# A four-layer GraphSAGE stack on one core: rests of a layer's first two chunks moved into the third place, PSUM banks that alternate by layer, and a layer's first loads ahead of the last stores

## Chip, core and metric

The kernel runs on one core of a Trainium2 chip. The metric is the device time of one execution in microseconds (us); lower is better. Engines are called by the names of the profile: PE (TensorE), PEld (its weight loads), DVE (VectorE), ACT (ScalarE), POOL (GpSimd) and SP (the engine whose queue issues almost all DMAs here).

## Reference

Input: node features x (3125 x 256, float32), 50000 edges (src, dst) and the weights of four layers. What is computed, cut to what matters:

```
def sage_conv(x, src, dst, Wl, Wr, b):
    agg = segment_sum(x[src], dst)          # sum over incoming edges
    deg = segment_sum(1, dst)
    return (agg / max(deg, 1)) @ Wl + x @ Wr + b

h = relu(layernorm(x))
h = relu(sage_conv(h, Wl1, Wr1, b1))        # 256 -> 256
h = relu(sage_conv(h, Wl2, Wr2, b2))        # 256 -> 128
h = relu(sage_conv(h, Wl3, Wr3, b3))        # 128 -> 256
return x + sage_conv(h, Wl4, Wr4, b4)       # 256 -> 256
```

## The kernel before

**Data.** The edges are first turned into a dense matrix of counts (source node by destination node, float16, resident in SBUF as `counts`). This is spread over the first half of the execution and runs into layer 1. From then on a layer's aggregation is a matrix product: `H` (features of all 25 tiles of 128 source nodes, in float16, a high and a low part) against `counts`. Layer 2 aggregates after its left map was already applied ("narrow"), so it has 128 features there.

**Chunks and places.** The destination nodes are cut into seven chunks: six of 512 nodes and a last one of 53. They are worked through in `ORDER` = 5, 6, 4, 3, 2, 1, 0; the position in that order is called place q (0 to 6). So place 0 is a full chunk, place 1 is the short chunk of 53 nodes, and places 2 to 6 are full chunks. For one place PE issues 25 tiles of sums (`add_sources`, L1720): two matmuls a tile (high and low part) in layers 2 and 3, four in layer 4, each with 512 columns, or 53 in place 1. They accumulate in one of two PSUM banks, `agg_ps` (bank 0) or `window_ps` (bank 1). Before the change, places 0, 2, 4, 6 use bank 0 and places 1, 3, 5 use bank 1, in each of layers 2 to 4; layer 1 uses bank 0 throughout.

**The rest of a place.** What follows a place's sums is called its rest:

- DVE multiplies the sums by 1/degree into `aggT` (`scale_agg`, L1200). It needs the tile `rdeg`, loaded from DRAM for each place, and `aggT` free, that is the map of the place before done.
- PE applies the layer's map (`lin`: L1682 in layers 2 and 3, L1665 in layer 4) to `aggT` and to `selfT`, the chunk's own features, loaded from DRAM (`load_self`, L642).
- In layer 2, DVE adds the sums to the map (L1301). ACT applies bias and relu into `newT` (L1412); SP stores `newT` to DRAM (`store_new`, L663).
- In layers 2 and 3 ACT makes the float16 high part (L1425), DVE the low part (L1207), PE transposes both (`turn`, L1707; once in layer 2, twice in layer 3), DVE copies the result to `newH` (`copy_turned`, L1219), and SP stores it (`store_H`, L670) for the next layer's `H`.
- In layer 4, DVE adds x (L1289) and SP stores the output.

PE has one in-order stream, written out by hand: the map and turn of place q-1 stand among the sums of place q, after fixed tiles. `rest(l, q)` lists them: map after tile 6, turn after tile 18 in layer 2; map after 6, turns after 16 and 22 in layer 3; map after tile 4 in layer 4. With this rule the rest of place 0 stands among the 53-column sums of place 1, and the rest of place 1 among those of place 2.

**Change of layer.** Place 0 of a layer consumes the `H` that the layer before has made. Its 25 tiles are taken in `ORDER`, and the rest of the last place of the old layer stands among them (`REST_AT`, the map before tile 0). SP issues, in this order: reload of `H` for all chunks but the last one (after all sums of the old layer, L745); `store_new` and `store_H` of place 6; the reload of the last chunk of `H` (L750), once its store has landed; then, once every `hT_stored` of the old layer is there, `load_self(0)` (L642), `load_rdeg(0)` (L648), and in layer 2 six late weight loads (`Wr2`, `Wl3`, `Wr3`, `b4`, `Wl4`, `Wr4`: L719 to L725), which all count on one semaphore, `late_loaded`. The map of place 0 in layer 2 waits for all six.

After that, `after(q)` on SP waits for the map of place q, then issues `load_self(q+1)`, `load_rdeg(q+1)` (once `agg_scaled` allows), `store_new(q)` and `store_H(q)`.

Of the kernel before, what the change touches and what calls it, by code (L numbers as in the profile page):

```python
# [26 lines left out]
def sage_stack_kernel(nc, x, src, dst, Wl1, Wr1, b1, Wl2, Wr2, b2, Wl3, Wr3, b3, Wl4, Wr4, b4, out):  # L27
# [13 lines left out]
    P = 128  # L41
# [3 lines left out]
    NT = -(-N // P)  # L45
# [4 lines left out]
    NCH = NFULL + 1  # L50
# [106 lines left out]
    for at_, (w, i) in enumerate(STEP):  # L157
        if i:
            continue
        k = STEPS[w]  # L160
# [62 lines left out]
    with ctx:  # L223
# [6 lines left out]
        def sem(name):  # L230
            return ctx.enter_context(nc.semaphore(name))
# [221 lines left out]
        degree_done = sem("degree_done")  # L453
        degree_inverted = sem("degree_inverted")
        degree_turned = sem("degree_turned")
        late_loaded = sem("late_loaded")
        rdeg_made = sem("rdeg_made")
        rdeg_stored = sem("rdeg_stored")
# [35 lines left out]
        CONSTS = CONSTS_TURN + 9  # L494
        LATE_KEYS = sum(r[4] > 1 for r in RUNS)
        LATE_CONSTS = len(FOURS) + 1
        LATE = 16 * 6
        x4 = newH[:, :, :, :].rearrange("p t h f -> p (t h f)").bitcast(f32).rearrange("p (t f) -> p t f", t=TPC)
        FULL = (CH, TPC)
        LAST = (TAIL, 1)  # L500
# [15 lines left out]

            return full * q - (full - last if not isinstance(q, int) or q > 1 else 0)

        def over_places(eng, do):

            do(1, 1)
            do(2, 0)
            with eng.Fori(1, NCH // 2) as i:
                do(2 * i + 1, 1)
                do(2 * i + 2, 0)

        def chunk_cols(c, n):
            return bass.ds(c * CH, n)
# [56 lines left out]
        def _(sp):  # L585
# [45 lines left out]
                store_h0T(j)  # L631

            for l in (1, 2, 3, 4):
                if l > 1:
                    sp.wait_ge(hT_stored[l - 1], 16 * NCH)

                def load_self(q):
                    c = chunk_at(q)
                    n, t = size_of(c)
                    if l == 1 and isinstance(q, int) and q <= 2:  # L640
                        wait_h0T(sp, *((q,) if q < 2 else ()))
                    sp.dma_start(selfT[:, 0:SELF[l], 0:n], hT_d[l - 1][:, 0:SELF[l], chunk_cols(c, n)]  # L642
                                 ).then_inc(self_loaded[l], 16)

                def load_rdeg(q):
                    c = chunk_at(q)
                    n, t = size_of(c)
                    sp.dma_start(rdeg[:, 0:n], rdeg_d[0:1, chunk_cols(c, n)].broadcast_to([P, n])  # L648
                                 ).then_inc(rdeg_loaded[l], 16)
# [34 lines left out]
                def load_x4(q):  # L684
# [4 lines left out]
                    else:  # L689
                        sp.dma_start(x4[0:n, 0, :], x[c * CH:N, :]).then_inc(x4_loaded, 16)  # L690

                def after(q, last=False):

                    sp.wait_ge(lin_done[l], both(q + 1, LIN[l], 1 if l == 4 else LIN[l]))
                    if not last:
                        load_self(q + 1)
                        if l > 1:
                            sp.wait_ge(agg_scaled[l], AGG[l] * (q + 1))
                            load_rdeg(q + 1)
                    if l == 1 and isinstance(q, int) and q == 0:  # L700
                        for j in range(3, NCH):
                            store_h0T(j)
                    if l < 4:
                        store_new(q)
                        store_H(q)
                    else:
                        store_out(q)
                        if not last:
                            load_x4(q + 1)

                load_self(0)
                if l > 1:
                    if l == 2:
                        sp.wait_ge(rdeg_stored, 16 * NCH)
                    load_rdeg(0)
                if l == 2:


                    sp.dma_start(Wr2_sb, Wr2.rearrange("(k p) n -> p k n", p=P)).then_inc(late_loaded, 16)  # L719
                    for i, w in enumerate((Wl3, Wr3)):  # L720
                        sp.dma_start(W3[:, i, :], w).then_inc(late_loaded, 16)
                    sp.dma_start(b4rows, b4.rearrange("(o n) -> o n", o=1).broadcast_to([P, D])
                                 ).then_inc(late_loaded, 16)
                    for i, w in enumerate((Wl4, Wr4)):
                        sp.dma_start(W14[:, i, :, :], w.rearrange("(k p) n -> p k n", p=P)  # L725
                                     ).then_inc(late_loaded, 16)
# [142 lines left out]
        def _(dve):  # L869
# [423 lines left out]
            for l in (2, 3, 4):  # L1293
                def place(q, bank):
                    n, t = size_of(chunk_at(q))
                    scale_agg(l, q, bank)
                    if l == 2:
                        dve.wait_ge(lin_done[2], q + 1)
                        if not isinstance(q, int) or q > 0:
                            dve.wait_ge(hT_stored[2], 16 * q)  # L1300
                        v.tensor_tensor(newT[:, 1, 0:n], lin_ps[:, 0, 0:n], aggT[:, 0, 0:n], ALU.add  # L1301
                                        ).then_inc(summed, 1)
                    for h in range(TURNS[l]):
                        low_part(l, q, h)
                        copy_turned(l, q, h)
                    if l == 4:
                        add_out(q)

                place(0, 0)
                over_places(dve, place)  # L1310


        @block.scalar
        def _(act):
# [193 lines left out]
            for l in (2, 3):  # L1508
                def place(q, bank):
                    relu(l, q)  # L1510
                    for h in range(TURNS[l]):
                        high_part(l, q, h)

                place(0, 0)
                over_places(act, place)


        @block.tensor
        def _(pe):
# [128 lines left out]
            def lin(l, q):  # L1648
# [2 lines left out]
                pe.wait_ge(agg_scaled[l], AGG[l] * (q + 1))  # L1651
                pe.wait_ge(self_loaded[l], 16 * (q + 1))
                if l == 2 and isinstance(q, int) and q == 0:
                    pe.wait_ge(late_loaded, LATE)
                if l == 4:
                    if not isinstance(q, int) or q > 0:
# [163 lines left out]
            def rest(l, q):  # L1820
# [3 lines left out]
                        3: {6: [lambda: lin(3, q)], 16: [lambda: turn(3, q, 0)], 22: [lambda: turn(3, q, 1)]},  # L1824
                        4: {4: [lambda: lin(4, q)]}}[l]


            for l in (2, 3, 4):
                def place(q, bank):
                    between = rest(l, q - 1)  # L1830

                    if not isinstance(q, int) or q > 1:
                        pe.wait_ge(agg_scaled[l], AGG[l] * (q - 1))
                    for k in range(NT):
                        add_sources(l, q, bank, k, k == 0, k == NT - 1)
                        for do in between.get(k, []):
                            do()

                pe.wait_ge(agg_scaled[l - 1], AGG[l - 1] * NCH)
                tiles = [(c, k) for c in ORDER for k in range(c * TPC, min((c + 1) * TPC, NT))]
                left = [do for _, dos in sorted(rest(l - 1, NCH - 1).items()) for do in dos]
                for i, (c, k) in enumerate(tiles):
                    if i in REST_AT[l - 1]:
                        left.pop(0)()
                    pe.wait_ge(H_loaded[c], 16 * (l - 1))
                    add_sources(l, 0, 0, k, i == 0, i == NT - 1)
                over_places(pe, place)
            lin(4, NCH - 1)  # L1850


# [21 lines left out]
```

## Time and profile before

| what | value |
|---|---|
| median of 3 runs | 731.82 us (731.35 to 734.61) |
| the profiled execution's own time | 732.57 us |
| its span in the profile | 730.5 us |
| mean granted PE clock | 0.975 |
| PE busy | 671.8 us, 92% of the span |
| DVE, ACT, POOL busy | 292.2, 172.4, 31.1 us |
| layers 2, 3 and 4, start of place 1 to start of place 3 | 363.84 to 390.86, 457.27 to 480.69, 570.10 to 603.97 us |

How to read it: the profiled execution is a single one, with a span 2.07 us shorter than its own time and a time 0.75 us above the median. "Busy" for PE counts matmuls whose ends are modelled, so the distance from one start to the next is the better measure of what a matmul costs. Positions are in us from the start of the span. A granted clock of 1.00 is 2.4 GHz and 0.50 is 1.2 GHz. Layer 2's place 0 starts near 350 us, and layers 2 to 4 take the rest of the span.

### The profile page before, as it was taken

Reading aid. Unit: us, or ns where it says so; the run is one execution under the profiler, and the core shown is the slowest. Engines: PE = TensorE matmul, PEld = TensorE weight load, DVE = VectorE, ACT = ScalarE, POOL = GpSimd, SP = SyncE. Lnnn points to the kernel's source line nnn. Section 1 sums busy time; section 2 is a strip of 40 time slices with the busy share of each in tenths; the row PEclk is TensorE's granted clock in tenths of the full one; section 3 lists DMA queues with packets and bytes.
Section 4 is the critical chain, followed back from the end, with each engine's and each line's share of the span. In section 5 each row is a group of like instructions: output and inputs, shape, how many; then the busy total and the mean of one; then the engine's idle time right before and its main releaser. Section 6 shows DMA issues by size and latency. Waiting matters only on the chain.

```text
span 730.5 us, 11548 instructions
## 1 busy us (share of the span) xinstructions
PE 671.8 (92%) x4545; PEld 366.5 (50%) x4546; DVE 292.2 (40%) x826; ACT 172.4 (24%) x339; POOL 31.1 (4%) x80
## 2 busy tenths in 40 slices
PE   5578898999999999999959999899989999999997
PEld 4234555655554555644434444444434646556464
DVE  6898866686767757601011221212221101001001
ACT  4844753363624503210101010111120000000000
POOL 7000000000000000000000000000000110110110
PEclk9999999899999999999979999999999999999999
DMA  8000012300101001064423235222346222130230
GB/s 260 18 2 1 30 61 89 108 1 6 58 17 56 13 8 58 17 14 112 132 83 106 87 106 185 81 78 87 115 138 212 81 78 63 39 102 20 80 100 29
DMA packets 39425, 53.50 MB, mean 73 GB/s; under 512 B 8558, under 2 KB 21519, under 8 KB 39377
## 3 DMA queue, kind: packets, MB, share of 16 engines
q1 hardware_dynamic: 39260, 52.59, 23.5%
q8 instruction: 33, 0.54, 0.3%
q10 hardware_dynamic: 116, 0.24, 0.1%
q14 instruction: 16, 0.12, 0.1%
HBM read 31.86 MB, written 20.97 MB: 72 GB/s over the span
## 4 chain that ended last, share of the span: by engine, by line
PE 84%; DVE 7%; ACT 3%; DMA 3%; issue 2%; POOL 1%; SPq 1%; DVEq 0%; POOLq 0%; ACTq 0%
PE agg_ps L1720 39%; PE window_ps L1720 12%; PE lin_ps L1643 6%; PE window_ps L1599 6%; PE lin_ps L1665 6%; PE lin_ps L1682 4%; PE lin_ps L1739 2%; DVE early L1146 2%; PE turn_ps L1707 2%; PE lin_ps L1690 2%; ACT counts L1373 1%; DMA H_d<-newH 1%; DMA W<-in_L_gnn_Wr_dram 1%; DMA H<-H_d 1%; PE degree_ps L1751 1%
## 5 line engine op out<-in xcount | busy, mean ns | idle before, releaser
L1720 PE MATMUL agg_ps<-counts,H 128*128 128x512 f16 (+2 forms) x1500 | 355.0, 374 | 2.1 <-DMA H<-H_d 2.1
L1720 PEld LDWEIGHTS agg_ps<-counts,H 128*128 128x128 f16 x1500 | 130.0, 99 | 119.1 <-issue 12.9
L1146 DVE TENSOR_TENSOR early<-early 128x512 f16<-128x512 bf16 (+2 forms) x466 | 153.6, 390 | 38.6 <-PE window_ps L1599 37.2
L1373 ACT ACTIVATE counts<-window_ps 128x400 f16<-128x400 f32 x196 | 96.3, 505 | 133.5 <-PE window_ps L1599 129.6
L1599 PEld LDWEIGHTS window_ps<-early 128*128 128x128 f16 x892 | 70.0, 100 | 112.7 <-issue 30.7
L1599 PE MATMUL window_ps<-early 128*128 128x100 f16 (+1 forms) x892 | 100.3, 223 | 24.4 <-DVE early L1146 14.3
L1720 PE MATMUL window_ps<-counts,H 128*128 (+1 forms) x600 | 96.2, 316 | 0.0
L1720 PEld LDWEIGHTS window_ps<-counts,H 128*128 128x128 f16 x600 | 45.6, 98 | 49.6 <-issue 4.1
L1200 DVE SCALAR_TENSOR_TENSOR aggT<-agg_ps,columns,rdeg 128x512 f32<-128x512 f32 (+1 forms) x30 | 20.5, 715 | 101.1 <-PE agg_ps L1720 89.8
L835 POOL TENSOR_TENSOR newH<-newH,early 128x256 f32<-128x256 f32 (+1 forms) x25 | 17.4, 725 | 680.9 <-DMA newH<-in_x_dram 680.9
L1219 DVE COPY newH<-turn_ps 128x1024 f16<-128x1024 f16 (+1 forms) x28 | 17.7, 632 | 58.6 <-PE turn_ps L1707 58.6
L1412 ACT ACTIVATE newT<-lin_ps,columns 128x512 f32<-128x512 f32 (+1 forms) x28 | 17.3, 633 | 96.9 <-PE lin_ps L1682 62.8
L1207 DVE SCALAR_TENSOR_TENSOR partsT<-newT,columns,partsT 128x512 f16<-128x512 f32 (+1 forms) x21 | 14.4, 684 | 53.6 <-ACT partsT L1425 53.0
L1682 PE MATMUL lin_ps<-selfT,early 128*128 128x512 f32 (+1 forms) x56 | 26.8, 583 | 6.8 <-DMA W<-in_L_gnn_Wr_dram 5.8
L1289 DVE TENSOR_TENSOR newT<-lin_ps,newH 128x512 f32<-128x512 f32 (+1 forms) x13 | 8.7, 671 | 56.4 <-PE lin_ps L1665 51.3
L1665 PE MATMUL lin_ps<-W,aggT 128*128 128x256 f32 (+1 forms) x100 | 25.9, 382 | 1.7 <-DVE aggT L1200 1.7
L1643 PE MATMUL lin_ps<-aggT,W 128*128 128x512 f32 (+1 forms) x56 | 25.8, 565 | 1.4 <-DVE aggT L1200 1.4
L1665 PE MATMUL lin_ps<-W,selfT 128*128 128x256 f32 (+1 forms) x100 | 25.7, 379 | 0.0
L1643 PE MATMUL lin_ps<-selfT,W 128*128 128x512 f32 (+1 forms) x56 | 25.5, 561 | 0.0
L1412 ACT ACTIVATE newT<-newT,columns 128x512 f32<-128x512 f32 (+1 forms) x7 | 4.7, 667 | 83.8 <-DVE newT L1301 83.8
L1200 DVE SCALAR_TENSOR_TENSOR aggT<-window_ps,columns,rdeg 128x512 f32<-128x512 f32 (+1 forms) x12 | 6.8, 589 | 39.9 <-PE window_ps L1720 36.7
L1707 PE MATMUL turn_ps<-ident,partsT 128*128 128x128 f16 (+1 forms) x200 | 16.5, 225 | 6.6 <-DVE partsT L1207 6.6
(159 smaller groups left out, 381.2 us busy)
## 6 DMA issues: line engine op xcount, KB each, us to landing
selfT<-hT_d SPq DMA_DIRECT2D x18, 512.0 KB, 4.3
hT_d<-newT SPq DMA_DIRECT2D x12, 512.0 KB, 4.2
rdeg<-rdeg_d SPq DMA_DIRECT2D x18, 256.0 KB, 4.2
counts<-in_x_dram SPq DMA_DIRECT2D x6, 512.0 KB, 8.3
hT_d<-counts SPq DMA_DIRECT2D x6, 512.0 KB, 3.2
H_d<-newH SPq DMA_DIRECT2D x12, 256.0 KB, 2.0
H<-H_d SPq DMA_DIRECT2D x12, 256.0 KB, 4.2
H_d<-newH SPq DMA_DIRECT2D x6, 512.0 KB, 2.6
```

The costliest lines, as they stand in the source:

```text
L835: nc.gpsimd.tensor_tensor(x4[0:q, i, :], x4[0:q, i, :], b4rows[0:q, :], ALU.add).then_inc(x4_biased, 1)
L1146: last = v.tensor_tensor(hot[:, group % GROUPS, 0:n * size].rearrange("p (r n d) -> p r n d", r=n, d=2), numbers_to[:, 0:size].rearrange(" ...
L1200: v.scalar_tensor_tensor(out=aggT[:, h, 0:n], in0=(agg_ps, window_ps)[bank][:, h, 0:n], scalar=unscale[:, l - 1:l], in1=rdeg[:, 0:n], op0= ...
L1219: v.tensor_copy(to, turn_ps[0:rows_, 0:2 * t, :].rearrange("p (t a) f -> p t a f", a=2)).then_inc(turn_copied[l], 1)
L1373: a.activation(counts[:, :, 2 * w * WIN:2 * (w + 1) * WIN].rearrange("p t (a w) -> p a t w", a=2), window_ps[:, FILL_AT[w] % 2, 0:2 * KEYS ...
L1412: a.activation(newT[:, h, 0:n], source, ACT.Relu, bias=bT[:, bias + h:bias + h + 1]).then_inc(relu_done[l], 1)
L1599: m(window_ps[:, at % 2, key0:key0 + keys], hot_src[:, group % GROUPS, r * P:(r + 1) * P], hot_key[:, group % GROUPS, r * keys:(r + 1) * k ...
L1643: last = m(lin_ps[:, h, 0:n], W14[:, i // 2, i % 2, h * P:(h + 1) * P], (aggT, selfT)[i // 2][:, i % 2, 0:n], start=(i == 0), stop=(i == 3))
L1665: last = m(lin_ps[0:rows_, g, i * D:(i + 1) * D], h, w, start=(j == 0), stop=(j == len(ops) - 1))
L1682: last = m(lin_ps[:, h, 0:n], w, r, start=(i == 0), stop=(i == len(ops) - 1))
L1707: last = nc.tensor.transpose(turn_ps[0:rows_, 2 * i + part, :], partsT[:, part, i * P:i * P + rows_], ident16[:, :])
L1720: last = m((agg_ps, window_ps)[bank][:, h, 0:n], H_of[:, k, part, h * P:(h + 1) * P], counts[:, k, chunk_cols(c, n)], start=first and part ...
```

## The change

What it does:

- **Rests of places 0 and 1.** In layers 2 to 4, place 1 has only its sums. The rest of place 0 and that of place 1 both stand among the sums of place 2, after the tiles that the new `first_rests` lists. From place 3 on nothing changes.
- **Banks.** `FIRST_BANK` gives the bank of places 0, 2, 4, 6 for each layer: 1 in layer 2, 0 in layer 3, 1 in layer 4. So the first place of a layer does not use the bank of the last place of the layer before. The wait ahead of place 0 asks for all scaled places of the old layer but the last; the wait for the last stands ahead of place 1. `REST_AT` is as before: the old layer's last map stands before tile 0 and waits for the last scaled place itself.
- **First loads.** `load_self(0)` and `load_rdeg(0)` of the next layer are issued in `first_loads`, after the last map of the old layer and ahead of `store_new(6)` and `store_H(6)`. For layer 2 the load of `Wr2` goes with them and has its own semaphore, `wr2_loaded`; the map of place 0 in layer 2 waits for that alone, and the five other late loads are waited for by the first map of layer 3.

The diff, cut where only a parameter is passed on:

```
+        wr2_loaded = sem("wr2_loaded")
...
-        LATE = 16 * 6
+        LATE = 16 * 5
...
-        def over_places(eng, do):
-
-            do(1, 1)
-            do(2, 0)
+        FIRST_BANK = [0, 0, 1, 0, 1]
+
+        def over_places(eng, do, first):
+
+            do(1, 1 - first)
+            do(2, first)
             with eng.Fori(1, NCH // 2) as i:
-                do(2 * i + 1, 1)
-                do(2 * i + 2, 0)
+                do(2 * i + 1, 1 - first)
+                do(2 * i + 2, first)
...
             for l in (1, 2, 3, 4):
-                if l > 1:
-                    sp.wait_ge(hT_stored[l - 1], 16 * NCH)
...
+                def first_loads(l):
+
+                    sp.wait_ge(hT_stored[l - 1], 16 * (NCH - 1))
+                    load_self(0, l)
+                    if l == 2:
+                        sp.wait_ge(rdeg_stored, 16 * NCH)
+                        sp.dma_start(Wr2_sb, Wr2.rearrange("(k p) n -> p k n", p=P)).then_inc(wr2_loaded, 16)
+                    sp.wait_ge(agg_scaled[l - 1], AGG[l - 1] * NCH)
+                    load_rdeg(0, l)
+
                 def after(q, last=False):
 
                     sp.wait_ge(lin_done[l], both(q + 1, LIN[l], 1 if l == 4 else LIN[l]))
+                    if last and l < 4:
+                        first_loads(l + 1)
                     if not last:
...
-                load_self(0)
-                if l > 1:
-                    if l == 2:
-                        sp.wait_ge(rdeg_stored, 16 * NCH)
-                    load_rdeg(0)
+                if l == 1:
+                    load_self(0)
+                else:
+                    sp.wait_ge(hT_stored[l - 1], 16 * NCH)
                 if l == 2:
 
 
-                    sp.dma_start(Wr2_sb, Wr2.rearrange("(k p) n -> p k n", p=P)).then_inc(late_loaded, 16)
...
                 pe.wait_ge(self_loaded[l], 16 * (q + 1))
                 if l == 2 and isinstance(q, int) and q == 0:
+                    pe.wait_ge(wr2_loaded, 16)
+                if l == 3 and isinstance(q, int) and q == 0:
                     pe.wait_ge(late_loaded, LATE)
...
+            def first_rests(l):
+
+                return {2: {2: [lambda: lin(2, 0)], 8: [lambda: turn(2, 0, 0)],
+                            13: [lambda: lin(2, 1)], 19: [lambda: turn(2, 1, 0)]},
+                        3: {2: [lambda: lin(3, 0)], 8: [lambda: turn(3, 0, 0)], 12: [lambda: turn(3, 0, 1)],
+                            15: [lambda: lin(3, 1)], 19: [lambda: turn(3, 1, 0)], 22: [lambda: turn(3, 1, 1)]},
+                        4: {2: [lambda: lin(4, 0)], 10: [lambda: lin(4, 1)]}}[l]
 
             for l in (2, 3, 4):
                 def place(q, bank):
                     between = rest(l, q - 1)
+                    if isinstance(q, int):
+                        between = first_rests(l) if q == 2 else {}
 
                     if not isinstance(q, int) or q > 1:
                         pe.wait_ge(agg_scaled[l], AGG[l] * (q - 1))
+                    else:
+                        pe.wait_ge(agg_scaled[l - 1], AGG[l - 1] * NCH)
                     for k in range(NT):
                         add_sources(l, q, bank, k, k == 0, k == NT - 1)
                         for do in between.get(k, []):
...
-                pe.wait_ge(agg_scaled[l - 1], AGG[l - 1] * NCH)
+                pe.wait_ge(agg_scaled[l - 1], AGG[l - 1] * (NCH - 1))
...
-                    add_sources(l, 0, 0, k, i == 0, i == NT - 1)
-                over_places(pe, place)
+                    add_sources(l, 0, FIRST_BANK[l], k, i == 0, i == NT - 1)
+                over_places(pe, place, FIRST_BANK[l])
```

## Rows read from the trace of the kernel before

**Rows 1.** The page's first part: busy time, share of the span, instructions.

```profile
PE 671.8 (92%) x4545; PEld 366.5 (50%) x4546; DVE 292.2 (40%) x826; ACT 172.4 (24%) x339; POOL 31.1 (4%) x80
```

**Rows 2.** Who waited for whom: us in total, times, longest.

```profile
PE lin_ps L1682 <- DMA W<-in_L_gnn_Wr_dram: 5.8, 1, 5.8
PE turn_ps L1707 <- DVE partsT L1207: 6.6, 4, 2.5
```

**Rows 3.** Timeline of PE, layer 2: start, us, instruction, [idle before].

```profile
363.84 0.51 PE L1720 MATMUL window_ps<-counts,H 128*128 128x53 f16 x14
370.12 3.75 PE L1682 MATMUL lin_ps<-selfT,early 128*128 128x512 f32 x4 [5.77 <-DMA W<-in_L_gnn_Wr_dram]
...
376.95 0.88 PE L1707 MATMUL turn_ps<-ident,partsT 128*128 128x128 f16 x8 [2.48 <-DVE partsT L1207]
...
390.86 3.19 PE L1720 MATMUL window_ps<-counts,H 128*128 x14
...
403.81 3.19 PE L1720 MATMUL agg_ps<-counts,H 128*128 x14
```

**Rows 4.** Chain that ended last, layer 2: start, us, what.

```profile
373.90 0.70 DVE newT L1301
...
382.54 0.38 PE lin_ps L1682 x4
...
388.10 0.23 PE turn_ps L1707 x2
...
395.76 5.18 PE window_ps L1720 x24
```

**Rows 5.** Timeline of PE, layer 3.

```profile
457.27 0.52 PE L1720 MATMUL window_ps<-counts,H 128*128 128x53 f16 x14
...
464.23 0.62 PE L1707 MATMUL turn_ps<-ident,partsT 128*128 128x128 f16 x8 [1.67 <-DVE partsT L1207]
...
466.51 1.03 PE L1707 MATMUL turn_ps<-ident,partsT 128*128 128x128 f16 x8 [1.36 <-DVE partsT L1207]
...
480.69 3.18 PE L1720 MATMUL window_ps<-counts,H 128*128 x14
...
495.81 3.19 PE L1720 MATMUL agg_ps<-counts,H 128*128 x14
```

**Rows 6.** Chain that ended last, layers 3 and 4.

```profile
457.54 0.76 DVE aggT L1200
...
471.59 0.83 PE lin_ps L1682 x8
...
578.57 2.01 PE window_ps L1720 x80
...
584.90 1.86 PE lin_ps L1665 x8
```

**Rows 7.** Timeline of PE, layer 4.

```profile
570.10 0.67 PE L1720 MATMUL window_ps<-counts,H 128*128 128x53 f16 x20
...
603.97 4.48 PE L1720 MATMUL window_ps<-counts,H 128*128 x20
...
632.46 4.48 PE L1720 MATMUL agg_ps<-counts,H 128*128 x20
```

**Rows 8.** Windows: length, busy of each engine, PEclk, DMA share, GB/s.

```profile
367.00:369.00 2.00, 0.00 (x0) 0.00 (x0) 0.00 (x0) 0.00 (x0) 0.00 (x0) 0.50 0.58 201
...
444.00:450.00 6.00, 5.94 (x30) 2.63 (x30) 1.49 (x3) 1.44 (x2) 0.00 (x0) 1.00 0.87 268
```

**Rows 9.** Timeline at the change from layer 2 to 3.

```profile
450.67 0.34 SPq L670 DMA_DIRECT2D H_d<-newH  x1
...
455.53 1.41 PEld L1720 LDWEIGHTS agg_ps<-counts,H 128*128 128x128 f16 x8 [0.50 <-DMA H<-H_d]
```

**Rows 10.** The page's DMA issues: count, KB each, us to landing.

```profile
hT_d<-newT SPq DMA_DIRECT2D x6, 256.0 KB, 4.0
rdeg<-rdeg_d SPq DMA_DIRECT2D x3, 26.5 KB, 3.1
```

More of the change, by code:

```diff
@@ L633, in _, with load_self @@
             for l in (1, 2, 3, 4):
-                if l > 1:
-                    sp.wait_ge(hT_stored[l - 1], 16 * NCH)
-                def load_self(q):
+                def load_self(q, l=l):
                     c = chunk_at(q)
@@ L643, in load_self, with load_rdeg @@
                                  ).then_inc(self_loaded[l], 16)
-                def load_rdeg(q):
+                def load_rdeg(q, l=l):
                     c = chunk_at(q)
@@ L1307, in place @@
                         add_out(q)
-                place(0, 0)
-                over_places(dve, place)
+                place(0, FIRST_BANK[l])
+                over_places(dve, place, FIRST_BANK[l])
         @block.scalar
@@ L1512, in place @@
                         high_part(l, q, h)
-                place(0, 0)
-                over_places(act, place)
+                place(0, FIRST_BANK[l])
+                over_places(act, place, FIRST_BANK[l])
         @block.tensor
```

## The prediction, made before the changed kernel ran

> **What bounds the kernel now.** I read the page's busy shares first: PE works 92% of the span, the next engine 40% [rows 1]. So the end comes earlier only where PE waits or runs slowly, or if it gets less to do. The change gives PE the same matmuls in another order, so the gain can only come from waits and from the clock. The list of waits then says which waits: PE stood 5.8 us once before a map of L1682, until a weight load had landed, and 6.6 us in four places before turns, until DVE had made the low part [rows 2]. The timeline says where. The 5.77 us lie 14 matmuls into place 1 of layer 2, and a wait of 2.48 us before the turn follows in the same place [rows 3]. Two more waits before turns, 1.67 and 1.36 us, lie in place 1 of layer 3 [rows 5]. All this is in place 1, whose sums have 53 columns: in layer 4, 80 of them take 2.01 us [rows 6], 25.1 ns each, against 5.18 us for 24 sums of 512 columns, 0.216 us each [rows 4]. So the 50 sums of place 1 in layer 2 or 3 last 1.26 us, and a map's rest of over 3 us cannot hide in them. In place 2, a tile of two sums lasts 0.43 us and 25 tiles 10.8 us. The reader is to see that a wait's cover is the length of the sums behind which it stands.
>
> **Layer 2.** From the start of place 1 to that of place 3 the kernel takes 390.86 - 363.84 = 27.02 us [rows 3]. What has to be done there: the 50 short sums, 1.26 us; a full place with one full map and turn, for which the distance between the next two places stands, 403.81 - 390.86 = 12.95 us [rows 3]; the short map, 0.38 us, and the short turn, 0.23 us [rows 4]. Together 14.82 us. The excess is 12.2 us: 5.77 + 2.48 of it PE stood idle, and the other 3.95 us are work that took longer than elsewhere. The clock says why: 0.50 of full, that is 1.2 GHz, inside the idle stretch [rows 8], and not back to 2.4 GHz at once. I expect both idle and slow parts to go.
>
> What takes their place: the map of place 0 now stands after tile 2 of place 2, the turn after tile 8. From the map's end (DVE's add starts 0.02 us behind it, at 373.90) to the turn at 376.95, the chain add, relu, high part, low part needed 3.05 us [rows 3, 4]. Six tiles cover 2.59 us. So a stall of 0.46 us stays. After: 14.82 + 0.46 = 15.28 us, a gain of 11.7 us.
>
> This holds only if the loads come in time. `Wr2`, `selfT` and `rdeg` of place 0 are now issued about 10 us earlier, behind the old layer's last map, and I count no wait for them. The map of place 1 stands after tile 13, 0.46 us stall, a turn and 11 tiles (4.7 us) behind the first map, over 5.5 us. Its `rdeg` needs two issues on SP's queue and 3.1 us to land [rows 10]; it fits with about 1 us to spare. DVE's add for place 1 must also wait until `newT` of place 0 is stored: relu ends about 1.5 us behind the map, the store lands 4.0 us later [rows 10], 5.5 us, against a short map that ends near 6.1 us. It fits, by 0.6 us. `rdeg` and `selfT` of place 2 are asked for only after tile 13, about 5 us ahead of the place's end; should they be late by a microsecond, the next map stands six tiles further on (3 us), so it costs nothing; without that cover it would cost its full lateness.
>
> **Layer 3.** Before: 480.69 - 457.27 = 23.42 us. After: 1.26 + 15.12 (480.69 to 495.81) [rows 5] + 0.83 for the short map [rows 6] + two short turns at 0.23 [rows 4] = 17.67 us. The first turn stands six tiles behind the map and needs less than in layer 2, as no add is in the chain. The two full turns stood 466.51 - 464.23 = 2.28 us apart when PE only waited [rows 5]; now four tiles (1.73 us) and the turn itself lie between. The stall is between 0 and 0.55 us; the turn fills most of it, and I take 0.1. A gain of 5.65 us.
>
> **Layer 4.** Before: 603.97 - 570.10 = 33.87 us; after: 2.51 for 100 short sums + 28.49 (603.97 to 632.46) [rows 7] + 1.86 for the short map [rows 6] = 32.86 us, a gain of 1.0 us. A tile here has four sums (0.86 us), so eight tiles between the maps cover the output's add.
>
> **Does place 2 start at once?** It waits for the scaled sums of place 0. In layer 3 DVE was done with them 457.54 + 0.76 - 457.27 = 1.03 us after place 1 had begun [rows 5, 6], and place 1 now lasts 1.26 us. No stall, by 0.2 us; in layer 4 there are two such operations and 2.5 us.
>
> **Banks.** Nothing. The old layer's last map still stands ahead of tile 0 and waits for the last scaled place itself, so PE stands there as before. The bound is zero from both sides: the matmuls are the same, and `window_ps` is free by then.
>
> **First loads on SP's queue and in the DMA engines.** Each change of layer now has `selfT` and `rdeg` (and `Wr2`) ahead of `store_new(6)` and `store_H(6)`, 0.77 MB. SP's own issue time is no matter: `store_H(6)` waits longer for its turn. But the bytes lie ahead of it. At the change from 2 to 3, the six windowed microseconds from 444 moved 1.61 MB at 268 GB/s and kept the DMA engines 0.87 busy [rows 8]; with 0.77 MB more they would be done at 444 + 2.38 / 0.268 = 452.9 us, behind the issue of `store_H(6)` at 450.67 [rows 9]. The last chunk's reload follows only on that store, and PE already stood 0.5 us in its weight loads for it [rows 9], so lateness is paid in full. Below: 0 us (the queue is drained as fast as it fills; then these 0.5 us might even go). Above: all of 0.77 MB at 268 GB/s, 2.9 us. I take 1.2 us, since 2.2 us of the backlog lie behind the issue of the store, and about one of these would have passed before its own bytes start. At the other two changes the store is issued longer after the reloads, and I take nothing there, with the same 2.9 us as upper bound.
>
> The Trainium skill, DMA: Bandwidth & Descriptors, section Queues, rings and completion order, says that an engine takes the descriptors of one ring in order and lands a semaphore's increment only after all its earlier writes. That speaks against putting the loads first: by it the store could not be reported ahead of them, and the 1.2 us would not be 0. No row here shows the two transfers in that order.
>
> **Sum.** 11.7 + 5.65 + 1.0 - 1.2 = 17.2 us. The profiled execution took 732.57 us, so 715.4; the median of the runs is 731.82, which gives 714.6. I say 715.0.
>
> **Rivals.**
> - *Late reload at each change of layer.* 2.9 us three times, in place of 1.2: 17.2 - 7.5 = 9.7 us gained, 722 us; partly, 717 to 722. For it: the 0.5 us that PE already stood; against: the first and third change leave room. 12%.
> - *The chains still stall in place 2.* Place 2 has two rests in one place and DVE takes both in order; the margins above are 0.6 and 1 us. If layer 2 keeps its 2.48 us instead of 0.46 and layer 3 its 3.03 instead of 0.1: 4.9 us less, 720; partly, 717 to 720. 10%.
> - *The clock falls at each place 1 for a short time*, since PE now has a run of short matmuls there and a place begins without a map. Layer 2's excess of slow work, 3.95 us, in all three layers: 727. Against: short sums ran at 25.1 ns in layer 4 and the next place at full speed. 4%.
> - *Nothing to be measured.* Both of the first two at their upper ends and some clock: 17.2 - 7.5 - 4.9 - 4 = 1, 731 to 732. 3%.
> - *Slower.* One mechanism: the clock stays at 1.2 GHz through place 2. Work that lasts 12.95 and 15.12 us in layers 2 and 3 would last twice that: 28 us more, 743. It decides once more than 17.2 us of full-speed work runs at half. For it: after the long idle it was at 0.50 [rows 8]. Against: that idle is what goes, and the page shows none as long elsewhere in these layers. 5%.
>
> The Trainium skill, TensorE: Matmul & The Clock Gate, Part 1, says the slow clock is the default and activity releases it. It is the rule behind the last rival; the trace agrees in so far as the idle stretch ends at 0.50.
>
> **How the numbers follow.** My forecast, 712 to 718, has 66%. The range 712 to 720 takes in the bounds of the stalls, the second rival and a third of the first: 66 + 10 + 4 = 80%. About 0.5% is what a measurement of this kernel can tell from no change, so under 728.2 is faster: 66 + 12 + 10 + 4 = 92%; same 3%; slower 5%.
>
> **What the profile after would show.** Layer 2, place 1 to 3: about 15.3 us and no wait for a weight load; layer 3: 17.8; layer 4: 32.9; 50 short sums in about 1.3 us; a stall near 0.5 us before the first turn of layer 2's place 2; granted clock 1.00 at both places; PE waiting for `H<-H_d` some 1.2 us longer near the end of layer 3's place 0. I would be wrong if the clock fell all the same, if PE waited before tile 0 of place 2, or if the reload were late everywhere.

## The result and the profile after

The changed kernel took 716.24 us (median of 4 runs, 714.76 to 716.84), the kernel before, on the same chip, 733.11 us (median of 4, 731.35 to 734.61). The ratio is 0.9763, 95% interval 0.9731 to 0.9796: 2.4% faster, and 1.2 us above the 715.0 that were forecast. The profiled execution has a span of 713.8 us against 730.5, 16.7 us less; the prediction's sum was 17.2.

The busy shares on the page after, beside [rows 1]:

```profile
PE 664.6 (93%) x4545; PEld 363.3 (51%) x4546; DVE 292.6 (41%) x826; ACT 172.3 (24%) x339; POOL 30.8 (4%) x80
```

PE has the same 4545 matmuls, in 7.2 us less busy time. So only part of the 16.7 us is idle time; most of the rest is work that ran faster. (A small part is bookkeeping: the modelled end of the last matmul ahead of a wait lies about 0.16 us behind the point where the next one would have started, so each wait that goes takes that much "busy" time with it.)

PE's timeline in layer 2 after; it answers to [rows 3]:

```profile
363.85 1.42 PE L1732 MATMUL agg_ps<-counts,H 128*128 128x53 f16 x50
365.11 1.45 PE L1732 MATMUL window_ps<-counts,H 128*128 128x512 f16 x6
366.40 1.88 PE L1694 MATMUL lin_ps<-selfT,early 128*128 128x512 f32 x4
368.12 2.75 PE L1732 MATMUL window_ps<-counts,H 128*128 128x512 f16 x12
371.36 0.62 PE L1719 MATMUL turn_ps<-ident,partsT 128*128 128x128 f16 x8 [0.49 <-DVE partsT L1217]
...
379.44 3.19 PE L1732 MATMUL agg_ps<-counts,H 128*128 x14
```

Place 1 is one run of 50 short sums, 1.26 us from its start to that of place 2. The map starts without a wait, and the one wait left is 0.49 us before the turn. From place 1 to place 3: 379.44 - 363.85 = 15.59 us, where 27.02 us stood.

The granted clock in the windows of the same stretch (columns as in [rows 8]), where the kernel before had 0.50:

```profile
367.00:369.00 2.00, 2.00 (x8) 0.71 (x8) 0.68 (x1) 0.00 (x0) 0.00 (x0) 1.00 0.00 0
369.00:371.00 2.00, 1.87 (x9) 0.66 (x7) 0.46 (x2) 1.44 (x2) 0.00 (x0) 1.00 0.23 61
371.00:373.00 2.00, 1.64 (x14) 1.05 (x15) 1.21 (x3) 0.00 (x0) 0.00 (x0) 1.00 0.30 110
```

PE's timeline in layer 3 and 4 after, beside [rows 5, 7]:

```profile
432.41 1.95 PE L1694 MATMUL lin_ps<-selfT,early 128*128 128x512 f32 x4 [0.99 <-DVE aggT L1210]
...
445.23 1.90 PE L1732 MATMUL agg_ps<-counts,H 128*128 128x512 f16 x8 [1.23 <-DMA H<-H_d]
446.97 1.41 PE L1732 MATMUL window_ps<-counts,H 128*128 128x53 f16 x50
...
464.93 3.19 PE L1732 MATMUL window_ps<-counts,H 128*128 x14
...
554.34 2.68 PE L1732 MATMUL agg_ps<-counts,H 128*128 128x53 f16 x100
556.86 2.75 PE L1732 MATMUL window_ps<-counts,H 128*128 128x512 f16 x12
...
587.31 4.48 PE L1732 MATMUL agg_ps<-counts,H 128*128 x20
```

Layer 3, place 1 to 3: 464.93 - 446.97 = 17.96 us. Layer 4: 587.31 - 554.34 = 32.97 us. In layer 3, too, part of what went is slow work, which the prediction doesn't mention. In the trace of before, after the waits of 1.67 and 1.36 us, the clock was at 0.50, and 14 sums of place 2 took 471.43 - 467.54 = 3.89 us, where they take 3.02 at full speed:

```profile
467.54 4.04 PE L1720 MATMUL agg_ps<-counts,H 128*128 128x512 f16 x14
471.43 0.32 PE L1682 MATMUL lin_ps<-aggT,early 128*128 128x53 f32 x2
...
467.00:469.00 2.00, 2.00 (x14) 1.12 (x12) 0.87 (x2) 0.00 (x0) 0.00 (x0) 0.50 0.00 0
```

The line at 445.23 is the cost: eight sums on H's last chunk waited 1.23 us for its reload.

### The profile page after: what moved, and what is told of

Its sections match the earlier page's. It is cut to its first block, busy times and chain, and to the rows that moved or that the text cites. A ratio compares the mean times of both kernels' runs of the same rounds, so it can differ in the third digit from the quotient of the medians.

```text
span 713.8 us, 11549 instructions
## 1 busy us (share of the span) xinstructions
PE 664.6 (93%) x4545; PEld 363.3 (51%) x4546; DVE 292.6 (41%) x826; ACT 172.3 (24%) x339; POOL 30.8 (4%) x80
## 4 chain that ended last, share of the span: by engine, by line
PE 85%; DVE 7%; ACT 3%; DMA 3%; issue 2%; POOL 0%; DVEq 0%; SPq 0%; ACTq 0%; POOLq 0%
PE agg_ps L1732 32%; PE window_ps L1732 20%; PE lin_ps L1653 6%; PE window_ps L1609 6%; PE lin_ps L1677 6%; PE lin_ps L1694 4%; PE lin_ps L1751 2%; DVE early L1156 2%; PE turn_ps L1719 2%; PE lin_ps L1702 2%; ACT counts L1383 1%; DMA H<-H_d 1%; DMA H_d<-newH 1%; PE degree_ps L1763 1%; PE degree_ps L1533 1%
## 5 line engine op out<-in xcount | busy, mean ns | idle before, releaser
L1732 PE MATMUL agg_ps<-counts,H 128*128 128x512 f16 (+2 forms) x1350 | 290.3, 349 | 1.2 <-DMA H<-H_d 1.2
L1732 PE MATMUL window_ps<-counts,H 128*128 (+2 forms) x750 | 157.9, 366 | 1.9 <-DMA H<-H_d 1.9
L1732 PEld LDWEIGHTS agg_ps<-counts,H 128*128 128x128 f16 x1350 | 104.7, 99 | 81.5 <-issue 9.3
L1732 PEld LDWEIGHTS window_ps<-counts,H 128*128 128x128 f16 x750 | 68.9, 98 | 84.7 <-issue 4.4
L1210 DVE SCALAR_TENSOR_TENSOR aggT<-agg_ps,columns,rdeg 128x512 f32<-128x512 f32 (+1 forms) x27 | 17.0, 659 | 67.5 <-PE agg_ps L1732 61.9
L1229 DVE COPY newH<-turn_ps 128x1024 f16<-128x1024 f16 (+1 forms) x28 | 17.7, 633 | 51.6 <-PE turn_ps L1719 51.6
L1210 DVE SCALAR_TENSOR_TENSOR aggT<-window_ps,columns,rdeg 128x512 f32<-128x512 f32 (+1 forms) x15 | 10.4, 716 | 68.0 <-PE window_ps L1732 68.0
L1694 PE MATMUL lin_ps<-selfT,early 128*128 128x512 f32 (+1 forms) x56 | 24.9, 547 | 1.0 <-DVE aggT L1210 1.0
L1677 PEld LDWEIGHTS lin_ps<-W,aggT 128*128 128x128 f32 (+1 forms) x100 | 18.6, 187 | 5.1 <-DVE aggT L1210 1.6
```

What stands on the lines that cost most here:

```text
L1210: v.scalar_tensor_tensor(out=aggT[:, h, 0:n], in0=(agg_ps, window_ps)[bank][:, h, 0:n], scalar=unscale[:, l - 1:l], in1=rdeg[:, 0:n], op0= ...
L1229: v.tensor_copy(to, turn_ps[0:rows_, 0:2 * t, :].rearrange("p (t a) f -> p t a f", a=2)).then_inc(turn_copied[l], 1)
L1677: last = m(lin_ps[0:rows_, g, i * D:(i + 1) * D], h, w, start=(j == 0), stop=(j == len(ops) - 1))
L1694: last = m(lin_ps[:, h, 0:n], w, r, start=(i == 0), stop=(i == len(ops) - 1))
L1732: last = m((agg_ps, window_ps)[bank][:, h, 0:n], H_of[:, k, part, h * P:(h + 1) * P], counts[:, k, chunk_cols(c, n)], start=first and part ...
```

## Experiments

Of every run, the time from one stage to the next is compared, because the part ahead of the change moves from one execution to the next: layer 1's last map starts between 342.4 and 347.1 us in the traces of kernels that are the same up to there. Columns of this table: the distance from place 1 to place 3 in layers 2, 3 and 4; the last map of layer 2 to place 1 of layer 3 (place 0 of layer 3 with its waits); layer 1's last map to the end of the span; all in us. Then the median and its ratio to the kernel before, which ran beside each group of runs again (medians 732.43 to 733.25 us). In "last map later" the map itself moves, so the two columns that count from it are left open.

| run | L2 | L3 | L4 | place 0 of L3 | to the end | median | ratio (95%) |
|---|---|---|---|---|---|---|---|
| before | 27.02 | 23.42 | 33.87 | 13.44 | 387.2 | 733.11 | 1 |
| after | 15.59 | 17.96 | 32.97 | 14.56 | 370.3 | 716.24 | 0.9763 (0.9731 to 0.9796) |
| rests back | 20.09 | 23.51 | 33.88 | 13.83 | 380.7 | 726.78 | 0.9915 (0.9899 to 0.9932) |
| loads back | 19.29 | 17.97 | 32.97 | 13.59 | 373.4 | 717.42 | 0.9782 (0.9762 to 0.9801) |
| loads back, one semaphore | 18.45 | 17.97 | 32.98 | 13.40 | 372.1 | 720.47 | 0.9824 (0.9806 to 0.9842) |
| banks back | 15.58 | 17.97 | 32.98 | 14.33 | 370.2 | 718.33 | 0.9804 (0.9782 to 0.9827) |
| loads behind at 2 to 3 | 15.59 | 17.97 | 32.98 | 13.39 | 369.1 | 715.21 | 0.9768 (0.9743 to 0.9792) |
| and turn at 10 | 14.92 | 17.97 | 32.97 | 13.35 | 368.4 | 715.37 | 0.9769 (0.9749 to 0.979) |
| last map later | 15.58 | 17.98 | 32.97 | - | - | 726.97 | 0.9934 (0.991 to 0.9958) |
| more bytes ahead | 15.59 | 17.97 | 32.97 | 15.97 | 371.7 | 717.67 | 0.979 (0.9768 to 0.9812) |
| after, again | 15.59 | 17.96 | 32.97 | 13.69 | 369.5 | 715.95 | 0.977 (0.9743 to 0.9797) |
| behind, turn at 10, early reload | 15.08 | 17.97 | 32.97 | 13.14 | 368.0 | 713.21 | 0.9743 (0.9718 to 0.9769) |

### Rests back

```
-                    if isinstance(q, int):
-                        between = first_rests(l) if q == 2 else {}
```

> The changed kernel with the rests of places 0 and 1 back at their old tiles (place 0's among place 1's short sums); first loads and banks stay changed. Theory 'cover' (a rest costs what the sums behind which it stands do not hide): layer 2, place 1 to 3, about 17.9 us (14.8 of work, 0.7 for the scaled sums, 2.45 before the turn), up to 20 if the clock falls; layer 3 back at 23.4, layer 4 at 33.9. Together 8.6 us over the changed kernel: about 725 us, 1 to 1.5% faster than before. Rival 'the weight load was all': the moved rests carry nothing, 716 us as the changed kernel.

Measured: 726.78 us, 0.85% faster than the kernel before, less than the 1 to 1.5% expected. Layer 3 and 4 are back at 23.51 and 33.88 us, layer 2 at 20.09, the upper end of what was expected. PE's timeline of layer 2:

```profile
365.51 1.99 PE L1694 MATMUL lin_ps<-selfT,early 128*128 128x512 f32 x4 [0.56 <-DVE aggT L1210]
367.34 0.77 PE L1732 MATMUL agg_ps<-counts,H 128*128 128x53 f16 x24
370.58 0.62 PE L1719 MATMUL turn_ps<-ident,partsT 128*128 128x128 f16 x8 [2.48 <-DVE partsT L1217]
371.04 0.47 PE L1732 MATMUL agg_ps<-counts,H 128*128 128x53 f16 x12
371.34 4.87 PE L1732 MATMUL window_ps<-counts,H 128*128 128x512 f16 x14
```

And its windows:

```profile
371.00:373.00 2.00, 2.00 (x21) 0.91 (x19) 0.96 (x2) 0.00 (x0) 0.00 (x0) 0.60 0.28 104
373.00:375.00 2.00, 2.00 (x7) 0.78 (x6) 0.00 (x0) 0.00 (x0) 0.00 (x0) 0.55 0.24 93
```

The 2.48 us before the turn are back to the hundredth, though no load is waited for: this wait is the chain's length less the sums that stand in between. The clock fell after it, and the 14 sums that follow took from 371.34 to the next map at 376.05, 4.71 us, against 3.02 us at full speed [14 x 0.216, rows 4]. The rival "the weight load was all" falls. The early loads alone (with the new banks, which "banks back" shows to do nothing) save layer 2 6.9 us (27.02 to 20.09) and the others nothing.

### Loads back

```
                     sp.wait_ge(lin_done[l], both(q + 1, LIN[l], 1 if l == 4 else LIN[l]))
-                    if last and l < 4:
-                        first_loads(l + 1)
...
                     sp.wait_ge(hT_stored[l - 1], 16 * NCH)
+                    first_loads(l)
```

> The changed kernel with the first loads of a layer issued where they were, behind the last stores and the last reload of H; Wr2 keeps its own semaphore. Theory 'cover': rdeg of layer 2's place 0 lands near 366 us, so place 2 there starts about 1.7 us late; the reload wait at the change from 2 to 3 falls from 1.2 to about 0.4 us. Net +0.6 us: about 717 us. Rival 'the early loads carry the layer-2 gain': PE waits 5 us or more again in layer 2 and the clock falls, 722 us or more. Rival 'the reload wait has nothing to do with the loads ahead of it': it stays at 1.2 us.

Measured: 717.42 us. Layer 3's place 0 is 1.0 us shorter, with a wait for H of 0.19 us in place of 1.23, if the changed kernel's first trace is taken; its second trace has 13.69 us and 0.23, and against that nothing is gained. Layer 2 is 3.7 us longer than after, not 1.7. PE's timeline:

```profile
364.57 1.41 PE L1731 MATMUL agg_ps<-counts,H 128*128 128x53 f16 x50
367.83 2.55 PE L1731 MATMUL window_ps<-counts,H 128*128 128x512 f16 x6 [1.85 <-DVE aggT L1209]
370.17 2.53 PE L1693 MATMUL lin_ps<-selfT,early 128*128 128x512 f32 x4
```

and the window:

```profile
369.00:371.00 2.00, 2.00 (x5) 0.85 (x4) 0.00 (x0) 0.00 (x0) 0.00 (x0) 0.50 0.16 56
```

The late `rdeg` costs about the wait that was expected: 1.85 us, or 2.0 from start to start (3.26 us between the places where 1.26 are needed). The other 1.7 us are the clock at 0.50: six sums took 2.34 us from start to start in place of 1.29, the map 2.37 in place of 1.72. So the expected 717 us was met by luck: from layer 1's last map to the end the trace is 3.1 us longer than that of the changed kernel, where 0.6 was expected. The traced execution was also the slowest of the four (719.33 us; the others 715.25 to 717.94) and had the lowest mean clock (0.980; the others 0.985 to 0.988), so the clock need not have fallen like this in the others.

### Loads back, and all late loads on the wait

```
                     pe.wait_ge(wr2_loaded, 16)
+                    pe.wait_ge(late_loaded, LATE)
```

> As the run with the loads back, and layer 2's first map waits for all late weight loads again. So only the rests and banks are changed. Theory 'cover': the map waits until about 370 us in place of 368, 1.9 us more than with the loads back; layer 2, place 1 to 3, about 19.2 us, 719 us in all; if the clock falls as before the change, up to 4 us more, 723. Rival 'each byte of the 5.77 us wait comes back': 722.5 plus the clock's 4, 726 us.

Measured: 720.47 us in the timed runs; in its trace layer 2 took 18.45 us, less than the run above:

```profile
370.24 1.47 PE L1732 MATMUL window_ps<-counts,H 128*128 128x512 f16 x6 [1.30 <-DVE aggT L1209]
372.87 1.96 PE L1694 MATMUL lin_ps<-selfT,early 128*128 128x512 f32 x4 [1.16 <-DMA W<-in_L_gnn_Wr_dram]
```

The wait for the weights is 1.16 us, near a fifth of the 5.77 us [rows 3], on the same loads. Not all of the difference is cover. The loads landed 5.34 us after the start of place 1 (372.87 - 367.53), against 6.28 before; of these PE spent 1.26 us on the sums of place 1 and 1.29 on three tiles of place 2, and it stood 1.30 us for the scaled sums, which need the late `rdeg`. So PE stood 2.46 us in two waits where it stood 5.77 in one. The clock stayed at 1.00 in every window from 363 to 379. The rival "each byte of the wait comes back" falls. The medians (720.5 against 717.4 us) and the traces (372.1 against 373.4 us to the end) order these two runs differently; one trace of each can't tell how often the clock falls in either. The medians don't decide it: in this run's trace layer 1's last map starts at 347.10 us, in the run's above at 344.11, so 3.0 us lie ahead of everything that the two runs differ in. The 719 us expected were near the 720.47 for that reason; layer 2 itself was 0.75 us shorter than expected.

### Banks back

```
-        FIRST_BANK = [0, 0, 1, 0, 1]
+        FIRST_BANK = [0, 0, 0, 0, 0]
...
-                pe.wait_ge(agg_scaled[l - 1], AGG[l - 1] * (NCH - 1))
+                pe.wait_ge(agg_scaled[l - 1], AGG[l - 1] * NCH)
```

> The changed kernel with bank 0 for places 0, 2, 4, 6 in every layer and the old wait ahead of place 0. Theory: the banks do nothing, since the old layer's last map stands ahead of tile 0 and waits for the same scaled place: 716 us, the waits before the last maps stay at 1.37, 0.99 and 0.96 us. Rival: the banks save the wait for the last scaled place, about 1 us at each change of layer: 719 us.

Measured: 718.33 us, 2 us over the changed kernel, with intervals that overlap. The stages decide: 370.2 us to the end against 370.3. The waits ahead of the three last maps are 1.37, 0.99 and 0.96 us in both kernels; two of them:

```profile
434.59 1.96 PE L1694 MATMUL lin_ps<-selfT,early 128*128 128x512 f32 x4 [0.99 <-DVE aggT L1210]
...
528.49 1.10 PE L1694 MATMUL lin_ps<-aggT,early 128*128 128x512 f32 x2 [0.96 <-DVE aggT L1210]
```

The banks alone do nothing, as the map in front of tile 0 waits for the same scaled place.

### The last map later

So that the banks could pay, the old layer's last map and turns were put two tiles later.

```
-        REST_AT = {1: (0, 4, 9), 2: (0, 8), 3: (0, 7, 11)}
+        REST_AT = {1: (2, 6, 11), 2: (2, 10), 3: (2, 9, 13)}
```

> The changed kernel, but the old layer's last map and turns stand two tiles later in place 0 (map after 2 tiles, turns shifted as well), so that the alternated banks could hide the wait for the last scaled place. Theory 'H is the limit': PE can't begin tile 0 until H's first chunk is reloaded, 4 us after the sums end; the map no longer fills that time, and the last chunk's store and reload come later by two tiles' time. Layer 2's, 3's and 4's place 0 each 1 to 3 us longer: 719 to 723 us. Rival 'banks pay once the map is moved': 1 us less at each change of layer, 713 us.

Measured: 726.97 us, ratio 0.9934 (0.991 to 0.9958). PE's timeline at the three changes of layer:

```profile
344.70 1.02 PE L1732 MATMUL window_ps<-counts,H 128*128 128x512 f16 x4 [2.85 <-DMA H<-H_d]
...
436.57 1.02 PE L1732 MATMUL agg_ps<-counts,H 128*128 128x512 f16 x4 [3.05 <-DMA H<-H_d]
...
535.41 3.57 PE L1732 MATMUL window_ps<-counts,H 128*128 128x512 f16 x8 [6.39 <-DMA H<-H_d]
```

Nobody waits for the scaled sums any more, and all wait for H: 2.85, 3.05 and 6.39 us. At the first two changes of layer this costs 2.4 us and 1.3 to 2.2 us (against the changed kernel's two traces), as expected. At the third it costs 6.9 us: behind the longest wait the clock was at 0.50, eight sums took 3.36 us from start to start and the map 2.74, 2.7 us more than at full speed, and the other 4.2 us are longer waits, beyond the 1 to 3 us expected. Behind the waits of 2.85 and 3.05 us the four sums took 0.86 us from start to start, full speed. The map in front of tile 0 fills the reload's time, and this is why the banks can't pay here.

### Bytes ahead of the last store: none, as after, and double

Three kernels on one question: does PE's wait for H's last chunk in layer 3's place 0 come from the loads that the change put ahead of `store_H(6)`? In the first, they go behind the reload at this one change of layer:

```
-                    if last and l < 4:
+                    if last and l in (1, 3):
                         first_loads(l + 1)
...
+                if l == 3:
+                    first_loads(l)
```

> The changed kernel, but at the change from layer 2 to 3 selfT and rdeg are loaded behind the last reload of H, as before the change. Theory 'bytes ahead': the last chunk's store and reload no longer queue behind 0.52 MB, PE's wait for the reload falls from 1.23 to about 0.1 us; rdeg still lands before place 1 begins, since place 0 ends 4 us later. 1.1 us off: about 715 us. Rival 'rdeg is late': place 2 of layer 3 starts 1 us late and nothing is won. Rival 'the wait comes from elsewhere': 1.23 us stays.

In the second, two more loads of 256 KB into halves that layer 3 doesn't use stand ahead:

```
                     load_rdeg(0, l)
+                    if l == 3:
+                        sp.dma_start(selfT[:, 1:2, 0:CH], hT_d[2][:, 0:1, chunk_cols(ORDER[0], CH)]
+                                     ).then_inc(extra_loaded[0], 16)
+                        sp.dma_start(aggT[:, 1:2, 0:CH], hT_d[2][:, 0:1, chunk_cols(ORDER[0], CH)]
+                                     ).then_inc(extra_loaded[1], 16)
```

> The changed kernel with 0.52 MB more (two unused loads of 256 KB into free halves) ahead of the last stores at the change from layer 2 to 3; the loads are extra work that the reference doesn't need. Theory 'bytes ahead': PE's wait for the last chunk of H in layer 3's place 0 grows by 0.52 MB at about 270 GB/s, 1.9 us, from 1.23 to 3.1 us: about 718 us, and the clock may fall. Rival 'fixed cost': the wait stays near 1.2 us, however many bytes are ahead.

The third is the changed kernel once more:

> The changed kernel once more, unaltered, beside the next run on the same chip. Theory: 716 us, PE's wait for H's last chunk at the change from 2 to 3 between 0.4 and 1.3 us, as it lay in the runs with the same bytes ahead (1.23, 0.44, 0.90). If it is 0 here, the bytes ahead are not its cause.

SP's timeline shows it best: `store_H(6)` (L670 or L671) is issued, and the reload (L760 and its like) goes out once that store has landed. First the loads behind:

```profile
438.36 0.34 SPq L670 DMA_DIRECT2D H_d<-newH  x1
440.40 0.34 SPq L762 DMA_DIRECT2D H<-H_d  x1
```

The changed kernel, its first trace:

```profile
434.48 0.38 SPq L642 DMA_DIRECT2D selfT<-hT_d  x1
434.90 0.43 SPq L648 DMA_DIRECT2D rdeg<-rdeg_d  x1
435.88 0.34 SPq L663 DMA_DIRECT2D hT_d<-newT  x1
439.14 0.34 SPq L670 DMA_DIRECT2D H_d<-newH  x1
442.53 0.34 SPq L760 DMA_DIRECT2D H<-H_d  x1
```

Its second trace:

```profile
438.11 0.34 SPq L670 DMA_DIRECT2D H_d<-newH  x1
440.57 0.34 SPq L760 DMA_DIRECT2D H<-H_d  x1
```

Double the bytes:

```profile
439.80 0.34 SPq L671 DMA_DIRECT2D H_d<-newH  x1
444.48 0.34 SPq L769 DMA_DIRECT2D H<-H_d  x1
```

From the store's issue to the issue of the reload, which SP sends as soon as the store has landed: 2.04 us with nothing ahead, as before the change (452.71 - 450.67; its first number is in [rows 9]); 3.39 and 2.46 us with 0.52 MB; 4.68 us with 1.04 MB. PE's wait follows: none, 1.23, 0.23 and 2.56 us (3.1 were expected for the last). "Rests back" and "banks back", whose queue is the same here, lie in between: 2.57 us with a wait of 0.44, 3.06 with 0.90. So the bytes are the cause and the wait is not fixed; but the same 0.52 MB cost anything between 0.2 and 1.2 us, which the one forecast number didn't say. What counts is what is still under way when the store is issued: in the changed kernel's first trace `rdeg` landed at 441.2 us, 2.1 us after the store's issue, in the second at 439.2, 1.1 us after it. In "last map later" the same two loads are ahead of the store, but they were issued 5.6 us after the reload of `H` began in place of 2.8, and the store took 2.03 us, as with nothing ahead. Moving the loads behind costs layer 3 nothing, 17.97 us. "Loads behind" has the ratio 0.9768, where the changed kernel has 0.9763 and 0.977: timing can't tell them apart. The gain is read from the stage, place 0 of layer 3: 13.39 us against 14.56 and 13.69.

### The turn two tiles later, and an earlier reload

With the loads behind at 2 to 3 kept, layer 2's first turn moves from tile 8 to 10:

```
-                return {2: {2: [lambda: lin(2, 0)], 8: [lambda: turn(2, 0, 0)],
+                return {2: {2: [lambda: lin(2, 0)], 10: [lambda: turn(2, 0, 0)],
```

> As the run before, and layer 2's first turn stands after tile 10 in place of 8. Theory 'cover': 8 tiles hide 3.4 us, the chain needs 3.05, so the 0.49 us stall (0.65 from start to start) goes; the second map after tile 13 still finds its input, as copy and scaling need 1.1 us and three tiles hide 1.3. About 714.5 us. Rival: the second map waits instead for copy, scaling or rdeg, and the sum is the same, 715.

Measured: layer 2 took 14.92 us, 0.67 less, and no wait stands before that turn. 715.37 us timed, the same as without it within the interval.

On top of this, H's reload after a layer was split, so that only the chunk of place 5 waits for place 5's store:

```
-                    sp.wait_ge(H_stored[l], 16 * (NCH - 1))
+                    sp.wait_ge(H_stored[l], 16 * (NCH - 2))
...
                     for c in ORDER[:-1]:
+                        if c == ORDER[-2]:
+                            sp.wait_ge(H_stored[l], 16 * (NCH - 1))
```

> The first loads behind the reload at the change from 2 to 3, layer 2's first turn after tile 10, and new: the reload of H for the five full chunks of places 0 and 2 to 4 and the short one is split, so that only the chunk of place 5 waits for place 5's store. Theory: the wait of 1.5 to 1.8 us before tile 0 of layer 4's place 0 goes, since its first chunk is asked for 1.5 us or more earlier; with the 1.1 and 0.6 us of the two other edits 3.2 us less than the changed kernel, 713 us. Rival 'bandwidth': in layer 4's place 0 the first chunk lands no earlier, and nothing is won beyond the 1.7 us.

Measured: 713.21 us, ratio 0.9743 (0.9718 to 0.9769), the lowest of all; the changed kernel in the same comparison 715.95 us, with an interval that overlaps (0.9743 to 0.9797). From layer 1's last map to the end: 368.0 against 369.5 us, 1.5 us less where 3.2 were expected. Layer 2 took 15.08 us. The first chunk in layer 4, by the chain of waits, in this kernel:

```profile
522.66 0.35 SPq L670
...
523.12 5.56 DMA H<-H_d
528.68 0.05 issue
```

and in the changed kernel's second trace:

```profile
523.43 2.67 DMA H_d<-newH
...
526.16 3.70 DMA H<-H_d
529.87 0.05 issue
```

The reload is asked for 3.0 us earlier by position, 2.3 us earlier counted from the start of the layer's last map (523.73 and 524.50 us), but it takes 5.56 us in place of 3.70, right behind the 0.5 MB store that it no longer waits for. PE's wait fell only from 1.74 to 1.32 us. The rival "bandwidth" was nearer.

## Why the prediction was right

- **Layer 2.** Forecast 15.28 us, a gain of 11.7; measured 15.59, a gain of 11.43. The excess of idle and slow work went, with the clock at 1.00. The stall before the turn was put at 0.46 us; its idle is 0.49, but from the start of the 12 sums to that of the turn it is 3.24 us where the sums need 2.59: 0.65. That is 0.19 of the miss of 0.31 us, and comes from setting DVE's chain, counted from the modelled end of a map, against sums counted from start to start. The clock was part of the gain as forecast: 3.95 us of slow work.
- **Layer 3.** Forecast 17.77, measured 17.96; the gain 5.46, not 5.65. The second full turn stands 2.26 us behind the first where its sums and the turn need 2.17, the 0.1 us that were forecast; each of the two short turns costs another 0.1, which wasn't. The prediction put the clock's fall in layer 2 alone; in layer 3, 1.4 of the 5.46 us are slow work as well (the second full turn, the four short sums behind it and the 14 sums of 512 columns). It did no harm, since the stage was costed as it would be afterwards. **Layer 4.** Forecast 32.86, measured 32.97.
- **The deadlines held.** In layer 2 the short map's add began 0.04 us after the map's modelled end (374.52; DVE at 374.56), so `newT` was stored in time; `rdeg` of place 1 and 2 was not waited for. Place 2 began 1.26 us after place 1.
- **First loads.** Forecast 1.2 us lost at the change from 2 to 3; measured 14.56 - 13.44 = 1.12 us in the first trace, 0.25 in the second, and 0.39 and 0.89 in the two runs with the same queue. The size came out right in the first trace by luck, and for a wrong reason in part: the text counted 0.77 MB, but `selfT` is 256 KB in layer 3, so 0.52 MB stood ahead. With that, its own arithmetic gives (1.61 + 0.52) / 0.268 = 7.95 us, a queue drained at 451.95, 1.3 us behind the store's issue. The size was off by a third, the mechanism held: the store landed 1.35 us later in one trace, 0.42 in the other. The prediction drew on the Trainium skill, DMA: Bandwidth & Descriptors, section Queues, rings and completion order, which says that a semaphore's increment lands only after all earlier writes of that DMA engine. The traces agree in direction: a store with loads ahead of it is reported later, 2.04, 2.46 to 3.39, 4.68 us, and in both traces of the changed kernel behind `rdeg`. They can't tell this order from transfers that merely share the same bandwidth.
- **The other two changes of layer** were put at nothing: layer 1's last map to place 1 took 20.35 us after, 20.49 before; layer 3's 27.81 in both.
- **Banks** at nothing: shown.
- **The sum.** 11.43 + 5.46 + 0.90 - 1.12 + 0.14 = 16.8 us, against 16.7 in the spans and 17.2 forecast. With the second trace's 0.25 us for the first loads it would be 17.7, so the forecast lies between two executions of the same kernel.
- **The parts overlap.** In layer 2 the early loads alone are worth 6.9 us, the moved rests alone 8.6 (27.02 to 18.45), both 11.4, since each hides some of the same wait. A sum over parts costed one by one would have come out 4 us too high; the forecast avoided that by building up the stage after and subtracting.
- **The rivals.** The slower one, a clock that stays low, didn't occur, nor did a short fall at each place 1. In layer 2 the clock did fall where an experiment left one wait of 1.85 or 2.48 us in place 1 or 2.

## What to carry to other kernels

Cost a moved dependent chain by the length of the independent work that stands behind it, at its new place: a wait is the chain less its cover, and short tiles (here 50 sums in 1.26 us) cover nothing. Cost the stage as it will be and subtract, rather than add up the parts. When a load is put ahead of a store, ask what waits for that store and divide the load's bytes, read from its own shape, by the queue's rate; in these runs that was an upper bound (0.52 MB at 268 GB/s are 1.9 us; the store landed 0.4 to 1.35 us later); if the waiting engine is the bound, put the load behind unless something needs it sooner.

## What was not expected of the hardware

- The clock's fall doesn't follow the length of a wait alone. One wait of 1.85 us in place 2 of layer 2 was followed by 0.50, and one of 1.84 us later in the same trace, before tile 0 of layer 4, left it at 1.00. Waits of 2.56 ("more bytes ahead"), 2.85 and 3.05 us ("last map later") left it at 1.00, one of 2.48 us ("rests back") did not. Nor do two waits near each other decide it: 1.30 and 1.16 us, 1.5 us apart, left it at 1.00, while before the change 1.67 and 1.36 us in layer 3, 0.9 us apart, were followed by 0.50. At 0.50 six sums took 2.34 us for 1.29, so the wait of 1.85 us cost 3.7. Which waits set it off stays open.
- The same transfers in the same order landed up to 0.9 us apart between two executions of the same kernel (2.46 and 3.39 us).
- A load that stands directly behind a store of 0.5 MB landed 5.56 us after its issue, where it took 3.70 us once the store was done (one trace of each).
